# Scatters of the last chunk but one placed behind the last gathers in the GpSimd list

## The reference, cut to what matters

```python
x = x + gnn(layernorm(x), src, dst, W, b)        # segment sum over 106250 edges, @ W, relu
xn = layernorm(x)                                # 6250 rows
w, e = top2(softmax(xn @ Wr + br))               # two experts of eight for each row
x = x + sum_k w[:, k] * (gelu(ln(xn)[e_k] @ W1[e_k] + b1[e_k]) @ W2[e_k] + b2[e_k])
```

## Time and profile before

| what | value |
|---|---|
| time, median of 3 executions | 1914.98 us (1914.52 to 1919.98) |
| span of the profiled execution (first to last instruction) | 1657.8 us |
| profiled execution's own time | not given; 257.2 us lie between its span and the median above |
| TensorE matmul busy | 1196.1 us, 72% of the span |
| GpSimd (POOL) busy | 1122.3 us, 68% |
| VectorE (DVE) busy | 951.9 us, 57% |
| ScalarE (ACT) busy | 595.5 us, 36% |
| gathers of edges (L830) | 832, 1001 ns each |
| scatters of rows (L858) | 98, 1004 ns each |
| adding scatters to the output (L890) | 44, 1657 ns each in the larger group of 38 |

### The profile page before, as it was taken

One profiled execution on the slowest core, in us unless ns is written; L12 is line 12 of the kernel. 1 busy time (PEld: TensorE's weight loads), 2 busy tenths in 40 slices (PEclk: granted clock), 3 DMA queues, 4 the chain that ended last, 5 costly groups with the idle time before them and its releaser, 6 DMA issues.

```text
span 1657.8 us, 26613 instructions
## 1 busy us (share of the span) xinstructions
PE 1196.1 (72%) x9098; PEld 988.4 (60%) x9098; DVE 951.9 (57%) x2502; ACT 595.5 (36%) x1169; POOL 1122.3 (68%) x1116
## 2 busy tenths in 40 slices
PE   6954556756358555995499649969848868688996
PEld 5954344535147224983388439848728746577995
DVE  8997457556435252657264744764645639465543
ACT  4954011111032003540345125515315335355663
POOL 5006777777777777777777777777777757864333
PEclk9999566557579557996799769979959969899998
DMA  6027866776485348974787569869659578999983
GB/s 187 1 97 264 270 218 214 220 230 180 129 261 163 110 117 262 293 241 130 251 283 246 144 202 320 272 193 300 188 185 307 171 239 240 279 305 289 255 243 93
DMA packets 262266, 356.06 MB, mean 215 GB/s; under 512 B 25476, under 2 KB 225702, under 8 KB 262132
## 3 DMA queue, kind: packets, MB, share of 16 engines
q1 hardware_dynamic: 195544, 205.39, 38.4%
q0 software_dynamic: 60224, 142.57, 30.1%
q10 hardware_dynamic: 6364, 6.40, 1.2%
HBM read 290.80 MB, written 65.38 MB: 215 GB/s over the span
## 4 chain that ended last, share of the span: by engine, by line
PE 36%; DMA 23%; POOL 18%; issue 9%; DVE 9%; ACT 3%; SPq 1%; POOLq 0%; DVEq 0%; ACTq 0%
DMA gt<-zt,srcI 12%; PE ps L1245 9%; PE ps L1260 9%; POOL gt L830 9%; PE ps L1159 8%; POOL xs L858 5%; DMA out<-gt,toks 4%; PE ps L1134 2%; PE ps L1170 2%; DVE ohl L1334 2%; PE ps L1197 2%; POOL out L890 2%; ACT h L1106 2%; POOL S L877 1%; DMA out<-acc 1%
## 5 line engine op out<-in xcount | busy, mean ns | idle before, releaser
L830 POOL DMA_INDIRECT gt<-zt,srcI x832 | 832.8, 1001 | 254.2 <-issue 180.1
L1159 PE MATMUL ps<-gt,S 128*128 128x257 f16 x1664 | 346.9, 332 | 199.6 <-DMA gt<-zt,srcI 198.4
L1159 PEld LDWEIGHTS ps<-gt,S 128*128 128x128 f16 x1664 | 202.9, 152 | 298.9 <-DMA gt<-zt,srcI 283.2
L1245 PE MATMUL ps<-xe,w1b 128*128 128x256 f16 x2688 | 345.5, 283 | 40.7 <-DVE xe L1650 19.9
L1260 PE MATMUL ps<-w2b,hT 128*128 128x256 f16 x2688 | 313.3, 274 | 13.4 <-DVE yb L1682 6.8
L1245 PEld LDWEIGHTS ps<-xe,w1b 128*128 128x128 f16 x2688 | 270.3, 101 | 85.3 <-DVE xe L1650 22.6
L1106 ACT ACTIVATE h<-ps,cb 128x256 f32<-128x256 f32 x448 | 227.5, 558 | 251.4 <-PE ps L1245 250.2
L1656 DVE SCALAR_TENSOR_TENSOR hT<-h,cb,hT 128x512 f16<-128x512 f32 x224 | 167.5, 749 | 235.1 <-ACT hT L1110 234.5
L1260 PEld LDWEIGHTS ps<-w2b,hT 128*128 128x128 f16 x2688 | 263.4, 98 | 46.9 <-issue 12.8
L1110 ACT ACTIVATE hT<-h,cb 128x512 f16<-128x512 f32 x224 | 161.7, 722 | 7.3
L1084 ACT ACTIVATE aT<-ps 128x256 f32<-128x256 f32 x98 | 37.5, 382 | 316.4 <-PE ps L1190 316.3
(11 more groups left out here) (261 smaller groups left out, 1253.0 us busy)
## 6 DMA issues: line engine op xcount, KB each, us to landing
w1b<-ws SPq DMA_DIRECT2D x56, 1024.0 KB, 6.6
w2b<-ws SPq DMA_DIRECT2D x56, 1024.0 KB, 9.2
ws<-w2b SPq DMA_DIRECT2D x16, 1024.0 KB, 5.3
xb<-xs SPq DMA_DIRECT2D x56, 260.0 KB, 8.0
gt<-zt,srcI POOLq DMA_INDIRECT x832, 3.8
ys<-yb SPq DMA_DIRECT2D x34, 256.0 KB, 7.4
w1b<-in_L_ffn_W SPq DMA_DIRECT2D x8, 1024.0 KB, 9.2
hT<-in_L_ffn_W SPq DMA_DIRECT2D x8, 1024.0 KB, 13.6
```

The lines of the kernel that those rows point to most:

```text
L830: e.indirect_dma_start(out=gt[:, i % NG, :], out_offset=None, in_=zt, in_offset=bass.IndirectOffsetOnAxis(ap=srcI[:, c, r:r + 1].bitcast(u ...
L1159: inst = e.matmul(PS[r % 2][:, 0:257], S[:, r % NS, :, c], gt[:, i % NG, part * 257:part * 257 + 257], start=(c == 0 and part == 0), stop= ...
L1245: inst = e.matmul(UP[n % 2][:, z * BS:(z + 1) * BS], w[:, l, kk, j * 128:(j + 1) * 128], xe[m % 2][:, k, kk, :], start=(kk == 0 and l == 0 ...
```

## The change

A step `xs` of chunk 6 is skipped in the planner as long as not all 832 gathers are emitted. Nothing else in the source differs; the planner's list is worked out anew from there on, for all engines. Chunks 0 to 5 and 7 are not touched by the condition itself.

```diff
                 if kind == "cg" and clock["POOL"] > s["now"] + 2.5:
                     continue
+                if kind == "xs" and arg[0] == LAST - 1 and at["fetch"] < n:
+                    continue
                 if kind in ("wa", "wc", "we", "nW", "lg", "r3") and s["bank"] > s["now"]:
                     continue
```

## The result

The kernel after takes 1926.05 us (median of 20 runs, 1919.43 to 1936.16), the kernel before 1918.84 us beside it (20 runs, 1913.60 to 1928.86). The ratio is 1.0037 [1.0022, 1.0052]: slower by some 7 us, where 14 us faster was forecast. 1926.05 is above the forecast's range.

A forecast was written before the change was run, and what follows sets the result against it. GpSimd's list was taken to pace from the first fetch-back, held by block 33's store; starting 10.5 us earlier, its last give came 13.8 us earlier, rounded to -14: span 1643.8 plus 257.2 gives 1901.0 us, range 1894 to 1908 (8 in 10: 1886 to 1917).

The forecast's parts named there:

- Gathers: Last seven gathers on GpSimd start 10.4 us earlier, at 1317.9; the last edge tile is ready at about 1332.9.
- Scatters: Chunk 6's eight scatters on GpSimd run from 1326.7 to 1337.1, 8.8 us later.
- The store of block 33: In SyncE's queue it goes ahead of block 34's load, at about 1321.7, landing by 1333.9; that load is 11.9 us later.
- Fetch-back: The first fetch-back on GpSimd starts without waiting, right behind the scatters, at 1337.1 instead of 1347.60: 10.5 us gained.
- Is the last chunk ready by then?: Last chunk's slots at about 1379 instead of 1396.70; TensorE's gap before block 38 closes, result 55 about 16 us earlier.
- GpSimd's path: Start 10.5 us earlier, same work to give 43 (1536.4), then gives; the last at 1634 instead of 1647.8: 13.8 us earlier.
- Theory E: Formed from later profiles, not forecast: gives and `sums` form one chain, some 262 to 272 us from give 34 to give 55.
- Blocks 34 to 37: Block 34's first product on TensorE at 1353.6, 7.6 us later; after four blocks, block 38 can start at 1404.9.
- What lies around the span (257.2 us ...) is taken as the same: Time outside the profiled span, up to the timed median, stays 257.2 us, since nothing there is touched.
- Rival 3: Slower: block 34 late, TensorE's gap stays, two gives fewer before the last `sums` cost 10 us; +5 to +10, 1922; chance 0.15.
- Rival 2: DMA engines full from 1403 to 1535, so earlier starts only queue: net -4 us (0 to -7), 1911; chance 0.20.

The follow-up runs named there:

- after_t2: The changed kernel, nothing edited, on a chip without stalls: ratio to the kernel before 0.9987 [0.9970, 1.0004].
- b_timed: The kernel before, nothing edited, timed and profiled on a chip without stalls: 1660.03 us (8 runs), ratio 0.9995.
- c_before: The kernel before, nothing edited, profiled again in a single execution: 1658.85 us.
- c_after: The changed kernel, nothing edited, profiled again in a single execution: 1662.96 us.
- e_gives: The changed kernel with gives 41 and 42 moved ahead of the last `sums` on GpSimd, nine in front again: ratio to before 1.0020 [1.0002, 1.0037].
- b_skip: The kernel before without the gives of blocks 45 and 47, all products still made: ratio to before 1.0013 [0.9993, 1.0032].
- after_t: The changed kernel, nothing edited, timed again on a slower chip: ratio to before 1.0026 [1.0002, 1.0049].
- e_skip: The changed kernel without the gives of blocks 45 and 47, all products still made: ratio to before 1.0000 [0.9982, 1.0017].
- e_turn: The changed kernel with block 34's transposes and x ahead of the last chunk's last node step (TensorE, VectorE): ratio to before 1.0051 [1.0035, 1.0068].
- e_movest2: The kernel before with chunk 6's scatters behind the last gather and block 33's store ahead of block 34's loads, nine gives in front: ratio 1.0011 [0.9988, 1.0035].
- b_g34: The kernel before with give 34 three fetch-backs later in GpSimd's list: ratio to before 1.0028 [1.0003, 1.0052].

## Why the prediction was wrong, step by step

**Right.** *Gathers*, *Scatters*, *The store of block 33*, *Fetch-back*, and, in direction, *Is the last chunk ready by then?*, seen where the stalls are absent, as in the trace that the forecast was read from. GpSimd in the changed kernel, `after_t2`, and then in the kernel before, `b_timed`:

```profile
1335.54 0.98 POOL L860 DMA_INDIRECT xs<-xrow,slI  x1 [0.30 <-issue]
1336.83 1.00 POOL L879 DMA_INDIRECT S<-ys,cidx  x1 [0.30 <-issue]
...
1372.82 1.02 POOL L860 DMA_INDIRECT xs<-xrow,slI  x1 [0.30 <-issue]
...
1382.29 0.98 POOL L860 DMA_INDIRECT xs<-xrow,slI  x1 [0.30 <-issue]
1383.80 1.61 POOL L892 DMA_INDIRECT out<-yb,toks  x1 [0.53 <-issue]
...
1516.47 2.01 POOL L901 DMA_DIRECT2D out<-acc  x1 [9.22 <-DMA out<-gt,toks]
1533.63 1.67 POOL L892 DMA_INDIRECT out<-gt,toks  x1 [15.14 <-DMA out<-acc]
...
1647.48 1.56 POOL L892 DMA_INDIRECT out<-gt,toks  x1 [2.06 <-DMA out<-gt,toks]
```
```profile
1349.04 0.94 POOL L877 DMA_INDIRECT S<-ys,cidx  x1 [11.15 <-DMA ys<-yb]
...
1383.21 1.83 POOL L890 DMA_INDIRECT out<-yb,toks  x1 [0.30 <-issue]
...
1399.16 1.07 POOL L858 DMA_INDIRECT xs<-xrow,slI  x1 [2.30 <-DVE slI L1445]
...
1529.76 2.00 POOL L899 DMA_DIRECT2D out<-acc  x1 [5.79 <-DMA out<-gt,toks]
1544.88 1.66 POOL L890 DMA_INDIRECT out<-gt,toks  x1 [13.12 <-DMA out<-acc]
...
1644.56 1.55 POOL L890 DMA_INDIRECT out<-gt,toks  x1 [2.83 <-DVE gt L1688]
```

The wait of 11.15 us is gone. Against gather 825 the first fetch-back is 10.9 us earlier (forecast 10.5), the slots 28.8 (forecast 17.7), the last `sums` 12.0. Result 55 is 10.6 us earlier, where the forecast had 16, so TensorE's gain was sized a third too high.

**The step that failed: *GpSimd's path*, "Start 10.5 us earlier, the same work up to give 43: 1536.4", and from it "the last at 1634".** The work up to give 43 is not the same, in two places.

The first place is in front of give 34. The new list has fourteen fetch-back steps and the eight scatters of chunk 7 there (1372.82 to 1382.29 above); the old one has thirteen steps and the scatters behind (1399.16). So from the first fetch-back to give 34 GpSimd takes 47.0 us where it took 34.2, and in both it hardly waits on the way (0.53 us against 0.30 in front of give 34 itself). The 10.9 us of the fetch-back are used up there, and give 34 comes 1.9 us later than in before.

The second place is behind it. The list has seven gives in front of the last `sums` and 15 behind, where it had nine and 13: behind the last `sums` the changed kernel takes 131.0 us (1516.47 to 1647.48), the kernel before 114.8. The 12.0 us won up to there are given back as 16.2 (14.0 and 13.6 in the single executions `c_before` and `c_after`). Theory E says that this giving back is no accident, since both stretches belong to one chain: 263.7 us from give 34 to the last give, against 261.4. `e_gives` supports it, where two gives changed sides and the end stayed. But the chain is not tight from its start: between give 34 and the last `sums` GpSimd's waits of over 1 us add up to 29.5 us in the changed kernel and 22.5 in before, and for the rest of 132.7 and 146.5 us it issues, fetch-backs for the most part. That the two totals are so near is measured, not explained. The Trainium skill says (DMA: Bandwidth & Descriptors, "Two DMAs through the same engine are not ordered") that only a completion semaphore tells that data have landed, so each dependent write must wait for the one before it. The trace agrees as far as it goes: the 14 steps behind give 41 in `after_t2` take 8.1 us each on average, of which GpSimd issues for 3.4.

**The second step: *Blocks 34 to 37*.** I counted the late load of block 34 as time of TensorE only, to be made up before block 38. There it was made up. But give 34 needs block 34's result, and its x stands behind all node steps of the last chunk in VectorE's new list. In `after_t2` the first product of block 34 is 4.3 us later than in before (forecast 7.6) and result 34 2.2 us; it is ready 0.3 us before GpSimd is through with the scatters, so there give 34 is held by its place in the list and result 34 would have been the next limit. On the slower chips give 34 does wait for result 34 (6.55 us in after, 14.96 in `b_skip`), and in the traces of after it is 5.5 to 10.3 us later than in `b_skip` (95.0), which has before's order. Measured there: 5 us (1.0026) and 7 us (1.0037) slower. The order alone doesn't account for that delay: in all five traces there that have the new order of the blocks (after, `after_t`, `e_gives`, `e_skip`, `e_turn`) ScalarE stalls for 11.0 to 19.3 us in front of its half of block 34's x, and in none of the four with the old order, so x comes 53 to 72 us behind gather 825 and not 34 to 38, and result 34 at 98 to 108 and not 91 to 97. That this stall is what makes the changed kernel slower there fits the traces and was not tested.

**The third: "What lies around the span (257.2 us ...) is taken as the same".** Only 1.4 us lie there. On the slower chips these 257 us are stalls inside the span, and they fall on the steps that the forecast moved: result 33 comes 33.3 us behind gather 825 and not 4.2, so the fetch-back gains 9.4 us only (37.2 against 46.6 in `b_skip`) and waits again, and of result 55's gain 0 to 12 us are left (363.8 and 351.7 against 364.2).

**The rivals.** Rival 3 had the sign and nearly the size (1922), and its words "two gives fewer in front of the last `sums` cost 10 us and eat the 10.5 of the fetch-back" describe the profile, as does its "gives 34 to 37 come behind more fetches". The rest of its mechanism was not the one: the slots came early and TensorE's gap closed, and putting two gives or all nine in front did not bring the gain back (`e_gives`, `e_movest2`). So that its size came out is in part luck. Rival 2, DMA full, was not tested by itself; its 4 us faster lie inside the interval of the chip without stalls (5.0 us faster to 0.7 slower), where they are not excluded.

**What stays open.** The cause of the 5 to 7 us on the slower chips, as said; whether an earlier give 34 alone makes the kernel faster, since no run had it clearly earlier than before; why it takes 261 us from give 34 to the end in one run and 275 in another; what share of `b_g34`'s loss goes by the fetch-backs; and, since no profile of the unchanged kernel was had on the slower kind of chip, its give 34 there is read from `b_skip`, which differs only behind the last `sums`.

## What to carry to other kernels

Find the serial chain that ends last and follow it back to its first link; here an edit that started nearly everything else earlier was worth nothing, because that link did not start earlier. Look for what holds the link: its place in the issuing engine's list as well as the result that it carries. When a kernel plans its own order, one condition moves steps on every engine: count what stands in front of and behind each joining wait in the new list before taking "the same work" as a term. And compare the profiled execution's span with the timed median first: 257 us between them were stalls, not surroundings.

## What the runs showed of the hardware that was not expected

The same program takes about 1660 us on some chips and about 1900 to 1920 on others: each of the five chips on which the experiments ran showed one kind only (one of them in three single executions); before had medians of 1662.85 (21 runs) and 1661.52 (29 runs) on two chips, 1899.97 (35 runs) and 1919.11 (36 runs) on two others. The first rows of before mix the two, a span of 1657.8 us and a median of 1914.98, and on which chips these were taken is not on record. The granted clock hardly differs (0.821 in `c_before` and 0.804 in after, of full speed on average), nor do bytes (356.06 MB in both) and busy times (TensorE 1196.1 and 1217.3 us). What differs is idle time with no releaser in the profile. The longest such waits (us in total, times, longest), first of after as shown:

```profile
ACT aT L1086 <- remote: 242.8, 22, 69.7
...
ACT h L1108 <- remote: 210.3, 48, 19.3
...
DVE hT L1658 <- issue: 137.5, 39, 20.1
PEld ps L1161 <- issue: 135.1, 65, 15.8
```

and of the same kernel as `after_t2`, where "remote" does not occur at all:

```profile
POOL gt L832 <- issue: 176.8, 578, 0.9
...
PEld ps L1192 <- issue: 20.8, 26, 1.8
```

On the one kind of chip engines stop for up to 20 us with nothing to wait for that the profile knows; on the other such waits are under 2 us for these lines. Not all of the first row is stall: in `after_t2` the same line waits 332.4 us in all, 52.4 at the longest, for TensorE. The stalls can fall on the same instruction on different chips: the one in front of ScalarE's half of block 34's x is 19.29 us in after, 19.22 in `e_gives` and 19.34 in `e_skip`, though 11.00 in `after_t`. The cause was not found. What was measured: the same change gives 0.9987 [0.9970, 1.0004] on the one and 1.0026 to 1.0037 on the other.
